# Router scores from symmetric sums and a centred gate, row variance on ScalarE, first weight splits on VectorE

## What is computed

```python
def layernorm(x): return (x - mean(x)) / sqrt(var(x) + 1e-5)      # per token
# gated attention map, 512 x 512 per batch, ctx is (4, 512, 128)
sim = ctx @ (Wq.T @ Wk) @ ctx.T / (sqrt(32) * 4)
mask = sim >= (153rd largest of its row)
A = sigmoid(sim) * mask
x = x + tanh(g_x) * ((1 - gamma) * layernorm(x) + gamma * (A + A.T) / 2)
# mixture of 8 experts, 2 per token
xn = layernorm(x)
w, idx = top2(softmax(xn @ gate.T)); w = w / sum(w)
out = x + tanh(g_f) * sum_k w[k] * (silu(xn @ w1[idx].T) * (xn @ w3[idx].T)) @ w2[idx].T
```

## Time and profile before

| | us |
|---|---|
| median of 3 runs (lowest, highest) | 840.82 (840.43, 841.42) |
| the profiled execution | 842.22 |
| its span, first to last instruction | 840.6 |

### The profile page before, as it was taken

How to read it: one execution, slowest core, us unless ns; L and a number is a source line. 1 busy time by engine, 2 the same in 40 slices (tenths; PEclk the granted TensorE clock), 3 DMA queues, 4 the chain that set the end, 5 groups by cost and what they waited for, 6 DMA issues and landing times.

```text
span 840.6 us, 10971 instructions
## 1 busy us (share of the span) xinstructions
PE 723.1 (86%) x3398; PEld 581.6 (69%) x3399; DVE 403.6 (48%) x912; ACT 285.4 (34%) x467; POOL 158.5 (19%) x202
## 2 busy tenths in 40 slices
PE   7200059986999999999999999999999999999996
PEld 3000037775788888888888888888888888888885
DVE  3888966745236522562238236522562282265222
ACT  4764434533126211441126116211441171153111
POOL 2393001565010110010011010110010011101010
PEclk9755567866999999999999999999999999999998
DMA  8700004466741632146112721632136118211111
GB/s 311 308 0 0 0 8 143 153 240 230 274 113 38 222 128 50 25 123 239 38 25 35 315 50 38 231 119 50 25 114 255 31 25 325 50 25 38 25 26 24
DMA packets 23150, 93.98 MB, mean 112 GB/s; under 512 B 2720, under 2 KB 2976, under 8 KB 19808
## 3 DMA queue, kind: packets, MB, share of 16 engines
q0 software_dynamic: 10992, 66.21, 25.4%
q1 hardware_dynamic: 12000, 27.62, 9.9%
q10 hardware_dynamic: 144, 0.00, 0.0%
HBM read 69.52 MB, written 24.30 MB: 112 GB/s over the span
## 4 chain that ended last, share of the span: by engine, by line
issue 71%; DVE 8%; PE 8%; POOL 4%; POOLq 3%; ACT 2%; DVEq 2%; DMA 1%; SPq 0%
POOL out L422 2%; PE bank L494 2%; PE bank L469 1%; PE bank L471 1%; POOLq L242 1%; ACT work L625 1%; PE bank L485 1%; POOLq L421 1%; DVE top L925 1%; DVE work L823 1%; PE bank L454 1%; DVE work L922 1%; DVE ln_stats L779 1%; POOL raw L430 1%; DVE work L919 1%
## 5 line engine op out<-in xcount | busy, mean ns | idle before, releaser
L526 PE MATMUL bank<-w_hi,xT_hi 128*128 128x512 f32 x560 | 225.7, 403 | 3.9 <-issue 3.9
L527 PE MATMUL bank<-w_hi,xT_lo 128*128 128x512 f32 x560 | 222.2, 397 | 0.0
L528 PE MATMUL bank<-w_lo,xT_hi 128*128 128x512 f32 x560 | 221.7, 396 | 0.0
L723 ACT ACTIVATE act_g<-bank 128x512 f32<-128x512 f32 x70 | 41.7, 596 | 337.0 <-PE bank L528 337.0
L526 PEld LDWEIGHTS bank<-w_hi,xT_hi 128*128 128x128 f32 x560 | 105.8, 189 | 28.0 <-issue 4.3
L528 PEld LDWEIGHTS bank<-w_lo,xT_hi 128*128 128x128 f32 x560 | 105.8, 189 | 25.9
L527 PEld LDWEIGHTS bank<-w_hi,xT_lo 128*128 128x128 f32 x560 | 105.9, 189 | 23.5
L526 PE MATMUL bank<-w_hi,hT_hi 128*128 128x512 f32 x280 | 115.2, 412 | 0.0
L1085 DVE TENSOR_TENSOR hT_lo<-bank,hT_hi 128x512 fp32r<-128x512 f32 x70 | 48.4, 692 | 139.1 <-ACT hT_hi L727 139.1
L1045 DVE TENSOR_TENSOR w_lo<-raw,w_hi 128x1024 fp32r<-128x1024 f32 x88 | 104.3, 1221 | 11.6 <-ACT w_hi L650 9.8
L528 PE MATMUL bank<-w_lo,hT_hi 128*128 128x512 f32 x280 | 109.8, 392 | 0.0
(11 more groups left out here) (188 smaller groups left out, 758.4 us busy)
## 6 DMA issues: line engine op xcount, KB each, us to landing
raw<-weights POOLq DMA_DIRECT2D x21, 2048.0 KB, 16.0
xtile<-routed SPq DMA_DIRECT2D x36, 260.5 KB
raw<-weights SPq DMA_DIRECT2D x3, 2048.0 KB, 16.2
w_hi<-weights POOLq DMA_DIRECT2D x2, 2048.0 KB, 13.2
xb_own<-x SPq DMA_DIRECT2D x3, 1024.0 KB, 8.9
out<-xb_own SPq DMA_DIRECT2D x3, 1024.0 KB, 5.0
routed<-pad SPq DMA_DIRECT2D x8, 260.5 KB
work<-ctxT SPq DMA_DIRECT2D x4, 256.0 KB, 4.8
```

Source lines behind the costliest of these rows:

```text
L526: nc.tensor.matmul(out_ap, hi, hi_w, start=start, stop=False)
L527: nc.tensor.matmul(out_ap, lo, hi_w, start=False, stop=False)
L528: return nc.tensor.matmul(out_ap, hi, lo_w, start=False, stop=stop)
L723: nc.scalar.activation(act_g[:, s, :], bank[GATE[s]][:, :], ACT.Silu).then_inc(silu_set[s], 1)
```

## The change

- *Scores.* With gate_c, the gate less the mean of each of its columns (column sums by TensorE, L494's kind, gate_c by VectorE), x1 times gate_c is the score times the row's deviation. x1 is base plus even part. The base part is transposed and multiplied before the sums are there (`base_scores`: batches 0 to 2 ahead of the masked counts, batch 3 later). The even part, c2 times the symmetric sum, is its own transpose as a 512 x 512 matrix, so `even_scores` multiplies it as it is. The choice needs no deviation; only the share does.
- *x1.* ScalarE copies the even part from PSUM (`even_rows`), VectorE adds it to x and takes the row sum with it; the variance comes from ScalarE's Square with a sum (`spreads`), and GpSimd's `row_scales` takes the scale from that.
- *Search.* Three tiles of a half are counted on VectorE, five on ScalarE; similar(3) comes ahead of count(0, 0).
- *First splits* move from GpSimd to VectorE (`first_low`), spread over part 4.
- *DMAs.* The load of raw group 1 waits for the base transposes (they use its buffer); GpSimd's two w_hi loads come behind both halves' deviations.
- *Ranks.* Five products a batch instead of fourteen.
- *Orders* of TensorE, ScalarE, GpSimd and VectorE in part 4 are rewritten.

```diff
-ON_VECTOR = 2
+ON_VECTOR = 3
...
+        even = [S[:, TB * k:TB * (k + 1), :] for k in (0, 1, 2, 1)]
+        xfT = [[raw[:, 1, D * k:D * (k + 1)] for k in range(2)]] * XBUFS + [[work[:, EARLY_AT + D * k:EARLY_AT + D * (k + 1)] for k in range(2)]]
...
+        scores_ps = [bank[6 + b % 2][:, 128 + TB * E * b:128 + TB * E * (b + 1)].rearrange("p (i e) -> p i e", e=E) for b in range(B)]
+        base_ps = [bank[7][:, 256 + TB * E * b:256 + TB * E * (b + 1)].rearrange("p (i e) -> p i e", e=E) for b in range(B)]
+        gate_ps = bank[6][:, 64:64 + E]
+        rank_ps = bank[5][:, 0:TB * E].rearrange("p (i e) -> p i e", e=E)
...
-            for q in range(2):
-                sp.dma_start(raw[:, q, :], w_groups[0, q]).then_inc(raw_in_0[q], 16)
+            sp.dma_start(raw[:, 0, :], w_groups[0, 0]).then_inc(raw_in_0[0], 16)
+            sp.wait_ge(base_mm, TB * XBUFS)
+            sp.dma_start(raw[:, 1, :], w_groups[0, 1]).then_inc(raw_in_0[1], 16)
...
-                    for q in range(2):
-                        pool.dma_start(w_hi[q][:, :, :].rearrange("p j n -> p (j n)"), w_groups[0, q]).then_inc(hi_in[q], 16)
+            for q in range(2):
+                pool.dma_start(w_hi[q][:, :, :].rearrange("p j n -> p (j n)"), w_groups[0, q]).then_inc(hi_in[q], 16)
...
+                then(nc.gpsimd.tensor_scalar(ln_v[:, 1, b, :], spread[:, TB * b:TB * (b + 1)], 1.0 / D, EPS, ALU.mult, ALU.add))
+                then(nc.gpsimd.tensor_tensor(ln_r[:, 1, b, :], ln_v[:, 1, b, :], rsqrt_pow[:, :], ALU.pow))
+                nc.gpsimd.tensor_tensor(ln_o[:, 1, b, :], ln_r[:, 1, b, :], minus_mean[:, b, :], ALU.mult).then_inc(ln2_set, 1)
             def route(b, tiles):
...
-            for q in range(2):
-                pool.wait_ge(hi_in[q], 16)
-                pool.wait_ge(raw_in_0[q], 16)
-                for j in range(OPS):
-                    nc.gpsimd.tensor_tensor(w_lo[q][:, j, :], raw[:, q, j * OPW:(j + 1) * OPW], w_hi[q][:, j, :].bitcast(F32),
-                                            ALU.subtract).then_inc(lo_set[q], 1)
-            scales(0, 2, ln1_stats, ln1_set)
-            scales(1, 0, ln2_stats, ln2_set)
-            scales(1, 1, ln2_stats, ln2_set)
+            base_scales(2)
+            row_scales(0)
+            row_scales(1)
             route(0, range(TB))
-            scales(0, 3, ln1_stats, ln1_set)
-            scales(1, 2, ln2_stats, ln2_set)
-            route(1, range(TB // 2))
-            scales(1, 3, ln2_stats, ln2_set)
-            route(1, range(TB // 2, TB))
+            base_scales(3)
+            row_scales(2)
+            route(1, range(TB))
+            row_scales(3)
             route(2, range(TB))
             route(3, range(TB))
...
+            def base_scores(b):
+                def transpose_tile(i):
+                    pe.wait_ge(base_set, TB * b + i + 1)
+                    if TB * b + i >= 1:
+                        pe.wait_ge(xfT_out, TB * b + i)
+                    for c in range(DC):
+                        last = nc.tensor.transpose(bank[4][:, c * P:(c + 1) * P], xb[b % XBUFS][:, i, c * P:(c + 1) * P], ident[:, :])
+                    last.then_inc(xfT_mm, 1)
+                transpose_tile(0)
+                for i in range(TB):
+                    if i + 1 < TB:
+                        transpose_tile(i + 1)
+                    pe.wait_ge(xfT_out, TB * b + i + 1)
+                    for c in range(DC):
+                        last = nc.tensor.matmul(base_ps[b][:, i, :], xfT[b][i % 2][:, c * P:(c + 1) * P], gate_c[:, c, :],
+                                                start=(c == 0), stop=(c == DC - 1))
+                    last.then_inc(base_mm, 1)
+            pe.wait_ge(consts, 1)
+            pe.wait_ge(gate_set, 1)
+            for b in range(XBUFS):
+                base_scores(b)
...
-                for i in tiles:
+                for i in range(TB):
                     if b > 0:
-                        pe.wait_ge(x1_set, TB * (b - 1) + i + 1)
+                        pe.wait_ge(even_out, TB * (b - 1) + i + 1)
...
+            def even_scores(b):
+                pe.wait_ge(even_out, TB * (b + 1))
+                pe.wait_ge(base_out, b + 1)
+                for i in range(TB):
                     for c in range(DC):
-                        last = nc.tensor.transpose(bank[4 + i % 2][:, c * P:(c + 1) * P], rows[b][:, i, c * P:(c + 1) * P], ident[:, :])
...
+                        last = nc.tensor.matmul(scores_ps[b][:, i, :], even[b][:, c, i * P:(i + 1) * P], gate_c[:, c, :],
                                                 start=(c == 0), stop=(c == DC - 1))
-                    last.then_inc(scores_mm, 1)
+                last.then_inc(scores_mm, 1)
...
                 pe.wait_ge(mask_set, b + 1)
-                for i in range(TB):
-                    nc.tensor.matmul(rank_ps[:, i, :], upper[:, :], mask[:, i, :], start=True, stop=False)
-                    for j in range(i):
-                        nc.tensor.matmul(rank_ps[:, i, :], ones_b[:, :], mask[:, j, :], start=False, stop=False)
-                    last = nc.tensor.matmul(rank_ps[:, i, :], ones_b[:, :], before[:, b, :], start=False, stop=True)
+                nc.tensor.matmul(rank_ps, upper[:, :], mask[:, :, :], start=True, stop=False)
+                for j in range(TB - 1):
+                    nc.tensor.matmul(rank_ps[:, j + 1:, :], ones_b[:, :], mask[:, j:j + 1, :].to_broadcast([P, TB - 1 - j, E]),
+                                     start=False, stop=False)
+                last = nc.tensor.matmul(rank_ps, ones_b[:, :], before[:, b:b + 1, :].to_broadcast([P, TB, E]), start=False, stop=True)
...
+            add_transposed(0)
+            add_transposed(1)
+            even_scores(0)
+            add_transposed(2)
+            even_scores(1)
+            ranks(0)
+            add_transposed(3)
+            ranks(1)
+            even_scores(2)
+            base_scores(3)
+            even_scores(3)
+            ranks(2)
...
             similar(2)
+            similar(3)
             count(0, 0)
-            similar(3)
             for k in range(SEARCH):
...
+            def xfT_copies(b):
+                for i in range(TB):
+                    act.wait_ge(xfT_mm, TB * b + i + 1)
+                    if TB * b + i >= 2:
+                        act.wait_ge(base_mm, TB * b + i - 1)
+                    nc.scalar.activation(xfT[b][i % 2], bank[4][:, :], ACT.Copy).then_inc(xfT_out, 1)
+                act.wait_ge(base_mm, TB * (b + 1))
+                nc.scalar.activation(base_score[:, b, :, :], base_ps[b], ACT.Copy).then_inc(base_out, 1)
...
+            def even_rows(b):
+                if b == 3:
+                    act.wait_ge(scores_mm, 2)
+                    act.wait_ge(x1_set, 2 * TB)
+                for i in range(TB):
+                    act.wait_ge(AA_mm, TB * b + i + 1)
+                    nc.scalar.activation(even[b][:, i, :], bank[i][:, :], ACT.Copy, scale=c2).then_inc(even_out, 1)
...
+            def spreads(b):
+                act.wait_ge(mean_set, b + 1)
                 if b == 2:
                     act.wait_ge(A_set, B)
                 if b == 3:
                     act.wait_ge(routed_in[0], 16 * 2 * TB)
                 for i in range(TB):
+                    t = TB * b + i
+                    last = nc.scalar.activation(rows[b][:, i, 0:D], xb[b % XBUFS][:, i, :], ACT.Square, bias=minus_mean[:, b, i:i + 1],
+                                                scale=1.0, accum_out=spread[:, t:t + 1])
+                last.then_inc(spread_set, 1)
...
+            xfT_copies(0)
+            xfT_copies(1)
+            late_base(2)
+            xfT_copies(2)
+            act.wait_ge(probe_final, 1)
+            for t in range(TILES):
+                if t == 3 * TB:
+                    act.wait_ge(half_counted, 1)
+                    sigmoids(0)
+                    sigmoids(1)
+                act.wait_ge(masked_set, t + 1)
+                last = count_masked(t)
+                if t == TILES // 2 - 1:
+                    last.then_inc(half_counted, 1)
+            last.then_inc(all_counted, 1)
+            even_rows(0)
             sigmoids(2)
+            spreads(0)
+            even_rows(1)
             normal_rows(0)
-            xfT_copies(0)
-            for b in range(1, B):
-                if b + 2 < B:
-                    sigmoids(b + 2)
-                shares(b - 1)
-                normal_rows(b)
-                xfT_copies(b)
-                if b == 1:
-                    late_base(2)
-                    late_base(3)
-            shares(B - 1)
+            sigmoids(3)
+            spreads(1)
+            shares(0)
+            even_rows(2)
+            normal_rows(1)
+            late_base(3)
+            xfT_copies(3)
+            spreads(2)
+            shares(1)
+            even_rows(3)
+            normal_rows(2)
+            spreads(3)
+            shares(2)
+            normal_rows(3)
+            shares(3)
...
```

(76 more changed lines are left out.)

168 lines of the change are left out of this document (62 added, 106 removed).

## The result

The changed kernel takes **853.67 us** (median; 852.09 to 854.44) beside 841.12 for the kernel before: ratio 1.0126, 95% interval 1.0065 to 1.0187, 12.5 us slower. The profiled execution took 852.09 around a span of 850.5, against 842.22 and 840.6. So the profiles account for a shift of 9.9 us, and the changed kernel's profiled execution happens to be its fastest. The forecast was 853.0 for the median and 854.4 for an execution like the profiled one of the kernel before.

What follows compares the result with a forecast made beforehand. The expert loop was taken as bound by TensorE matmuls, so the second tile's transpose sets the end. Mask_A(0) 8.0 us later plus 4.2 from there to that transpose gives 12.2, so 853.0 us median, range 845 to 861.

Steps and rivals of the forecast that it cites:

- What bounds it: Expert loop, bound by TensorE matmuls: whatever moves the second tile's transpose, at 214.56 us before, moves the end.
- Search: Stage up to probe_final: without GpSimd's splits, with a third VectorE tile, it ends at 70.5 us instead of 81.2.
- M: Start of mask_A(0) on VectorE, at 111.53 us before; forecast 119.6, 8.0 us later.
- The new stage on ScalarE: Base copies ahead of the masked counts: three batches take 36.0 us, to 101; all counted at 116.1, VectorE waits 19.
- Half clock: TensorE in the base stage: starts at 1.2 GHz and stays there, granted clock 0.50 throughout.
- Rival A: Base stage: clock rises, a tile costs 1.35 us, three batches 22.9 instead of 36.0; 835.4 us. Chance with D 0.13.
- Moved transfers, Square, the sum in x1: Moved loads hidden; ScalarE's Square with a sum 0.707 us; x1's added sum under 0.1 a tile.
- From M to the second tile: From mask_A(0) to the second tile's transpose, through routing: 107.2 us instead of 103.0.
- Sum: Whole kernel: 8.0 + 4.2 = 12.2 us slower; 853.0 for the median, 854.4 for a run like the profiled one.
- Rival D: Masked pass: base copies overlap it, all counted near 98, search gain kept; 835 to 840 us. Chance with A 0.13.
- Rival C: Second tile doesn't wait for routing, or choose(1) released earlier: 10.2 us slower or less, 849 to 851. Chance 0.15.
- Rival B: Clock falls already in even_scores(0), so A(2) starts at half clock: 3 to 7 us more, 856 to 860. Chance 0.17.

Runs made afterwards that it cites:

- e4: Changed kernel with the four splits of weight group 0 put back on GpSimd and off VectorE; 862.82 us.
- e5: Kernel before, with only the first expert's eight splits moved from GpSimd to VectorE; 828.66 us.
- e6: Changed kernel with two ScalarE reorderings: masked counts between base copies, and spreads(2) and shares(1) ahead of batch 3's base; 834.11 us.
- e10: e6 with two instead of three tiles of each half counted on VectorE; 833.80 us.
- e9: e5 with three instead of two tiles of each half counted on VectorE; 832.54 us.
- e3: Changed kernel with eleven unused 512-column products on TensorE between the first and second base transposes, to raise the clock; 851.28 us.
- e1: Changed kernel with ScalarE's sixteen masked counts put between the base copies of batches 1 and 2, the two sigmoids behind them; 840.18 us.
- e8: Changed kernel with GpSimd's row_scales(3) between the two halves of route(1), not behind all of it; 855.23 us.
- e2: Changed kernel with spreads(2) and shares(1) ahead of late_base(3) and xfT_copies(3) on ScalarE; 847.78 us.
- e7: e6 with even_rows(3) ahead of late_base(3) on ScalarE and even_scores(3) ahead of base_scores(3) on TensorE; 835.07 us.

## Why the prediction was right, and where it was not

- **What bounds it.** Right. The shift of the second tile's transpose, 9.8, is the shift of the span, 9.9.
- **Search.** Forecast 70.5, measured 69.14. That the gain is the removed GpSimd splits was shown from both sides (e4, e5). In e6's chain the third tile costs M nothing (e10), against 4.7 in my sum, and ScalarE's free time says the same for the changed kernel; it cost 4.3 alone (e9). That e5 without the third tile and without the reordered opening ends at 69.37 and the changed kernel at 69.14 says that opening and third tile about cancel.
- **The new stage on ScalarE.** Right in kind, 3.9 us too long, which is the mis-sized term (1.2 in ScalarE's start, 2.2 in the three batches, 0.2 in the counts, 0.3 between count and mask_A): all_counted forecast at 116.1, count started at 112.54; M 8.0 later forecast, 4.1 measured. ScalarE was free 1.2 earlier (63.67). The three batches took 33.8 (10.0, 10.9, 12.9), not 36.0. I had taken 1.87 and 3.7 for products, which are durations that run into the next row (65.27 + 1.71 is past 66.83); a tile costs the distance between starts, 2.45 here (65.27 to 67.72), and the last two tiles' products 3.28 (70.17 to 73.45). The earlier trace rows had 182.32, 184.93 and 187.39: distances of 2.61 and 2.46. The row was there and I read its duration.
- **Half clock.** Right: 0.50 throughout, and e3 shows that a warm start would have been lost. Rival A, chance 0.13, fell with the clock and not with its price: its 1.35 for a tile at full clock is near the 1.40 between two copies in e3 (66.10 to 67.50), and 5 us at full clock took 3.0 us off the stage.
- **Moved transfers, Square, the sum in x1.** Hidden or as priced: Square with a sum 0.71 (forecast 0.707), the sum's read 0.08.
- **From M to the second tile.** Forecast M + 107.2, measured M + 108.7. Point by point: ranks(0) M + 33.0 (33.8), first matmul M + 90.0 (forecast 90.5), wait in choose(1) 18.3 (20), places of batch 2 on time, last write M + 102.6 (forecast 102.2). What failed is the last step: not the tile but h was late. The second tile landed near 223.3 and TensorE came to it at 224.40. h was late because ScalarE could split the third weight group only from 212.78, 7.2 us after batch 2's last routing write had begun; I had followed the routing of batch 3 and the tile, and took the first expert block as 14.1 us of work with nothing to wait for. The two paths arrive 1.1 us apart, so the number hardly moved, but the step was wrong.
- **Sum.** 8.0 + 4.2 was forecast; the profile gives 4.1 + 5.7. The two mistakes partly cancel, and the median lies 1.6 above the profiled execution, which brings it to 0.7 us of the forecast. The forecast is therefore better than its working.
- **Rival D** (the change carries its search gain) is what e1 makes of it: 840.2, where D said 835 to 840. I excluded it by ScalarE's order, and that order is what the edit undoes.
- **Rival C** held in part: what comes last at the second tile is not the last routing write but h, and that by 1.1 us. **Rival B** did not occur in the profiled execution of the changed kernel; it did in those of e4 and e10, and in e8 one step later, in A(2).

Open: in e5 the second tile stands at M + 100.1 and in the kernel before at M + 103.0, with the same program after M but for the splits. Of these 3 us, 2.7 are there when route(3) begins (M + 83.5 against M + 86.2). Part of them is clock: the products of batch 2's last two tiles ran at full clock in e5 (1.97 us for 16), and in the kernel before the last eight took 1.87. The rest stays open.

## What to carry to other kernels

When work moves to an engine, read what stands behind it in that engine's program: here the saving of 11.9 us sat in front of a wait of 16.3 us, and the same instructions in another order gave 13.5 us back. Before taking a bundle of edits, price each alone: the one that moves work off GpSimd while VectorE does small instructions was worth 14 us by itself, and the rest, even with both stalls repaired, took 5.5 of them back. In a stage that alternates between engines, cost a step by the distance between starts, not by the duration of a row. And where an engine waits for two things at once, find out which came last before pricing either: a load that is issued late can still be done before the writes beside it.

## What was not expected of the hardware

A TensorE that went into the base stage at 2.4 GHz was at 1.2 GHz 5 us later, though busy in most of that time (e3). In the first expert block, 2.92 us of waiting for h stand between two levels of the clock: 1.00 before the wait, 0.58 over the 3.4 us after it. The window from 221.60 to 225.00 of the changed kernel:

```profile
221.60:225.00 3.40, 3.40 (x14) 2.72 (x13) 0.99 (x2) 0.60 (x1) 0.00 (x0) 0.58 0.24 71
```

The same happens in e2 and e6, which wait 2.88 and 3.44 us for the second tile and run at 0.66 and 0.55 over the next 3.6 to 3.8 us; with the fall behind the transpose and not before it, these two end 630 instead of 628 us after it. In e7, which waits 2.39 us there, the clock stayed at 1.00.

The same products met both levels of the clock: 32 of eight columns behind 16 us of symmetric sums ran at full clock in the changed kernel and in e6 (3.64 us), and in e4 (4.73) and e10 (4.57) the clock fell while they ran, with the same TensorE instructions in front of them.

From the start of batch 2's last routing write to the split that waits for it 7.2 to 7.7 us passed in the changed kernel, e1, e3 and e4, where the load of the third group's weights was issued 8.8 us before that write, and 3.0 in e2, where it was issued 16.8 us before. That the load slows the writes is argued from this, not tested.
